# State-space scan layer: the gate's PSUM read moved from VectorE to ScalarE, its multiply to GpSimd, and the output projection from step 7 to step 9

## The reference

```python
xi, z = split(xs @ W_in)                 # 64 + 64 channels
xc = silu(causal_conv4(xi) + conv_b)
dt_r, B, C = split(xc @ W_x)             # 2, 16, 16
dt = softplus(dt_r @ W_dt + b_dt)
def step(h, inp):                        # h: 64 channels x 16 states
    h = exp(dt * A) * h + dt * B * x
    y = sum_over_states(h * C)
y = y + xc * D_skip
y = y * silu(z)                          # the gate
out = x + y @ W_out                      # the output projection and the residual
```

## Time and profile before

| | |
|---|---|
| time, median of 3 runs | 3292.82 us (3287.38 to 3304.67) |
| the profiled execution's own time | 3303.62 us |
| its span | 3301.8 us |
| its mean granted PE clock | 0.936 |
| busy share of the span | PE 81%, DVE 76%, POOL 60%, ACT 58% |

### The profile page before, as it was taken

One profiled execution on the slowest core, in us unless ns is written; L12 is line 12 of the kernel. 1 busy time (PEld: TensorE's weight loads), 2 busy tenths in 40 slices (PEclk: granted clock), 3 DMA queues, 4 the chain that ended last, 5 costly groups with the idle time before them and its releaser, 6 DMA issues.

```text
span 3301.8 us, 39492 instructions
## 1 busy us (share of the span) xinstructions
PE 2664.9 (81%) x12378; PEld 799.5 (24%) x12378; DVE 2516.6 (76%) x2227; ACT 1904.1 (58%) x2344; POOL 1989.3 (60%) x1216
## 2 busy tenths in 40 slices
PE   4888878888788875468888888887888888888886
PEld 1233122331223311122222222222222222222221
DVE  4555545555555443349999999999999999999998
ACT  2524545245462333276767777776777777676772
POOL 1444233442335420248787888878788887878886
PEclk9989989899899987779999999999999999999998
DMA  3588315883138855556767676776757676676865
GB/s 139 191 285 245 101 39 160 291 253 116 52 124 292 259 148 128 120 116 157 168 144 175 141 176 148 162 165 149 172 140 180 144 168 160 152 169 142 183 140 118
DMA packets 276832, 537.44 MB, mean 163 GB/s; under 512 B 60024, under 2 KB 171072, under 8 KB 275824
## 3 DMA queue, kind: packets, MB, share of 16 engines
q1 hardware_dynamic: 242208, 450.82, 52.4%
q0 software_dynamic: 17568, 59.00, 6.5%
q10 hardware_dynamic: 16944, 26.17, 3.2%
HBM read 396.55 MB, written 139.33 MB: 162 GB/s over the span
## 4 chain that ended last, share of the span: by engine, by line
issue 17%; PE 17%; DVE 16%; ACT 3%; DMA 2%; POOL 1%; DVEq 0%; ACTq 0%; POOLq 0%; SPq 0%
DVE m_pb L420 10%; PE m_pb L270 5%; PE m_py L253 5%; DVE m_hs L425 4%; PE m_misc L218 3%; PE m_misc L237 2%; ACT m_da L377 1%; DMA m_dtb<-dt_rows 1%; PE m_misc L224 1%; PE m_py L249 1%; DVE m_gated L407 1%; DMA dt_rows<-m_dt 1%; ACT m_xg L300 1%; POOL m_hs L451 0%; DVEq L424 0%
## 5 line engine op out<-in xcount | busy, mean ns | idle before, releaser
L451 POOL TENSOR_TENSOR m_hs<-m_hs,m_cs 128x1024 f32<-128x1024 f32 x512 | 1205.5, 2359 | 343.1 <-DVE m_hs L425 343.1
L425 DVE TENSOR_TENSOR_SCAN m_hs<-m_da,m_pb 128x1024 f32<-128x1024 f32 x512 | 1170.7, 2287 | 31.6 <-ACT m_da L377 6.5
L270 PE MATMUL m_pb<-m_dtx,late 64*128 64x512 f32 x2048 | 597.8, 649 | 217.7 <-DVE m_hs L425 217.2
L377 ACT ACTIVATE m_da<-m_dtb,m_a_neg 128x1020 f32<-128x1020 f32 x512 | 579.7, 1143 | 286.2 <-DMA m_dtb<-dt_rows 189.5
L420 DVE TENSOR_TENSOR m_pb<-m_pb,m_bs 128x1024 f32<-128x1024 f32 x512 | 620.5, 1212 | 33.6 <-PE m_pb L270 33.3
L253 PE MATMUL m_py<-m_hs,late 128*64 128x512 f32 x2048 | 566.3, 632 | 62.3 <-POOL m_hs L451 62.3
L1372 POOL TENSOR_TENSOR t_xc<-t_xc,big 128x512 f32<-128x512 f32 x96 | 119.2, 1266 | 409.4 <-DVE big L1278 409.4
L1148 ACT ACTIVATE t_sq<-t_bank 128x512 f32<-128x512 f32 x192 | 105.5, 595 | 371.1 <-PE t_bank L1013 370.7
L270 PEld LDWEIGHTS m_pb<-m_dtx,late 64*128 64x128 f32 x2048 | 168.0, 188 | 614.2 <-DVE m_hs L425 546.4
L1252 DVE SCALAR_TENSOR_TENSOR t_xc<-t_bank,t_vec,t_xc 128x512 f32<-128x512 f32 x96 | 72.1, 751 | 283.1 <-PE t_bank L967 283.1
L948 PE MATMUL t_bank<-late,t_lwin 128*128 128x256 f32 x816 | 226.1, 414 | 52.8 <-ACT big L1163 34.7
(11 more groups left out here) (152 smaller groups left out, 3670.8 us busy)
## 6 DMA issues: line engine op xcount, KB each, us to landing
m_dtb<-dt_rows SPq DMA_DIRECT2D x512, 512.0 KB, 6.1
late<-right_factor POOLq DMA_DIRECT2D x102, 512.0 KB, 5.4
right_factor<-t_tile SPq DMA_DIRECT2D x192, 256.0 KB, 2.9
t_tile<-band_out SPq DMA_DIRECT2D x183, 256.0 KB, 4.1
band_out<-t_vwin SPq DMA_DIRECT2D x48, 512.0 KB
band_out<-t_vwin SPq DMA_DIRECT2D x48, 480.0 KB
dt_rows<-m_dt ACTq DMA_DIRECT2D x64, 256.0 KB, 3.3
t_xc<-in_x_cm SPq DMA_DIRECT2D x4, 2048.0 KB, 14.6
```

Source lines behind the costliest of these rows:

```text
L270: m = nc.tensor.matmul(pb[s % 2][:, half(n)], spread[rows, dg, :], dtx[par][rows, half(q)], start=True, stop=True)
L377: nc.scalar.activation(da[:, s % DA_RING, :, 1:T], dtb[s % DTB_RING][:, :].rearrange("p (r t) -> p r t", t=T)[:, :, 1:T], ACT.Exp, scale=a ...
L425: nc.vector.tensor_tensor_scan(hs[:, s % H_RING, :], da[:, s % DA_RING, :, :].rearrange("p r t -> p (r t)"), pb[s % 2][:, :], 0.0, ALU.mul ...
L451: nc.gpsimd.tensor_tensor(hs[:, s % H_RING, :], hs[:, s % H_RING, :], cs[q][:, :], ALU.mult).then_inc(hc_ready, 1)
```

## The change

The gate is cut in two. ACT copies the sums out of PSUM into `gated` ("take0" after its step 12, "take1" after step 4 of the next chunk), and POOL multiplies `gated` in place by silu(z) (gate0 after its step 13, gate1 after step 5 of the next chunk). A new semaphore `y_taken` links the two, and skip(0) on PE waits for it instead of `y_gated`. DVE no longer gates. PE's out moves from step 7 to step 9, behind bq0, and DVE's fin from step 8 to step 10. skip(1) still stands at PE's step 11 and still waits for `fin_done`.

```diff
         SHARES = {
             "tensor": {0: [(PRE, "x")], 2: [(OWN, "bq1")], 4: [(OWN, "cq1")], 5: [(PRE, "dt")], 8: [(PRE, "z")],
-                       7: [(POST, "out")], 9: [(PRE, "bq0")], 11: [(PRE, "cq0")]},
-            "scalar": {1: [(PRE, "silu_x")], 3: [(OWN, "bq1")], 5: [(OWN, "cq1")],
+                       9: [(PRE, "bq0"), (POST, "out")], 11: [(PRE, "cq0")]},
+            "scalar": {1: [(PRE, "silu_x")], 3: [(OWN, "bq1")], 4: [(POST, "take1")], 5: [(OWN, "cq1")],
...
-                       8: [(PRE, "sp_back"), (PRE, "sp_relu")], 9: [(PRE, "silu_z")], 10: [(PRE, "bq0")], 12: [(PRE, "cq0")],
+                       8: [(PRE, "sp_back"), (PRE, "sp_relu")], 9: [(PRE, "silu_z")], 10: [(PRE, "bq0")], 12: [(PRE, "cq0"), (OWN, "take0")],
...
-            "vector": {4: [(POST, "gate1")], 8: [(POST, "out")], 11: [(OWN, "gate0")]},
-            "gpsimd": {7: [(PRE, "loss0"), (PRE, "log0")], 8: [(PRE, "dt0"), (PRE, "loss1")],
+            "vector": {10: [(POST, "out")]},
+            "gpsimd": {5: [(POST, "gate1")], 13: [(OWN, "gate0")], 7: [(PRE, "loss0"), (PRE, "log0")], 8: [(PRE, "dt0"), (PRE, "loss1")],
...
                             if q == 0:
-                                pe.wait_ge(y_gated, 2 * k - 1)
+                                pe.wait_ge(y_taken, 2 * k - 1)
                             else:
                                 pe.wait_ge(fin_done, k)
...
+                def take(k, par, q):
+                    a.wait_ge(hc_used, S * k + DG * (q + 1))
+                    if q == 0 and not early(k, 1):
+                        a.wait_ge(o_ready, k)
+                    nc.scalar.copy(gated[:, half(q)], py[q][:, :]).then_inc(y_taken, 1)
...
-                    v.wait_ge(misc_used[q], use(k, "z") + 1)
-                    nc.vector.tensor_tensor(gated[:, half(q)], py[q][:, :], act[par][:, W + q * HALF:W + (q + 1) * HALF],
-                                            ALU.mult).then_inc(y_gated, 1)
...
+                def gate(k, par, q):
+                    g_.wait_ge(y_taken, 2 * k + q + 1)
+                    g_.wait_ge(misc_used[q], use(k, "z") + 1)
+                    nc.gpsimd.tensor_tensor(gated[:, half(q)], gated[:, half(q)], act[par][:, W + q * HALF:W + (q + 1) * HALF],
+                                            ALU.mult).then_inc(y_gated, 1)
```

More of the change, by code:

```diff
@@ L129, in mamba_layer @@
                  "b_ready", "da_ready", "u_done", "h_ready", "hc_ready", "hc_used",
-                 "y_gated", "o_ready", "fin_done", "stored")
+                 "y_taken", "y_gated", "o_ready", "fin_done", "stored")
         (xg_ready, sp_abs, sp_exp, sp_relu, sp_ln, sp_sum, sp_act_done, sp_loss, sp_log, dt_ready, dtx_ready,
          b_ready, da_ready, u_done, h_ready, hc_ready, hc_used,
-         y_gated, o_ready, fin_done, stored) = map(sem, names)
+         y_taken, y_gated, o_ready, fin_done, stored) = map(sem, names)
         misc_ready = [sem(f"misc_ready{i}") for i in range(2)]
@@ L290, in _ @@
                 a.wait_ge(shared.x_in, shared.X_LOADS)
+                def take(k, par, q):
[3 more added lines that the diff above has]
+                    nc.scalar.copy(gated[:, half(q)], py[q][:, :]).then_inc(y_taken, 1)
                 def pre(k, par, op):
-                    if op in ("xg0", "xg1"):
+                    if op == "take0":
+                        take(k, par, 0)
+                    elif op in ("xg0", "xg1"):
                         q = int(op[2])
@@ L389, in post @@
                 def post(k, par, op):
+                    if op == "take1":
+                        return take(k, par, 1)
                     a.wait_ge(fin_done, k + 1)
@@ L398, in _ @@
             def _(v):
[L399 to L405, removed]
-                    v.wait_ge(misc_used[q], use(k, "z") + 1)
-                    nc.vector.tensor_tensor(gated[:, half(q)], py[q][:, :], act[par][:, W + q * HALF:W + (q + 1) * HALF],
-                                            ALU.mult).then_inc(y_gated, 1)
-                def pre(k, par, op):
-                    gate(k, par, 0)
                 def steps(k, par, s, first, last):
@@ L428, in post @@
                 def post(k, par, op):
[L429 to L440, removed]
+                    v.wait_ge(o_ready, k + 1)
+                    if not early(k, 1):
+                        v.wait_ge(stored, 16 * G * k)
+                    nc.vector.tensor_tensor(fin[:, :].rearrange("p (n t) -> p n t", n=SUB),
+                                            py[1][:, :].rearrange("p (n t) -> p n t", n=SUB),
+                                            xm[:, :, bass.ds(SUB * k, SUB)].rearrange("p t n -> p n t"),
+                                            ALU.add).then_inc(fin_done, 1)
+                schedule(v, "vector", None, steps, post)
             @block.gpsimd
@@ L452, in steps @@
                                             ALU.mult).then_inc(hc_ready, 1)
+                def gate(k, par, q):
[3 more added lines that the diff above has]
+                                            ALU.mult).then_inc(y_gated, 1)
                 def pre(k, par, op):
+                    if op == "gate0":
+                        return gate(k, par, 0)
                     q = int(op[-1])
@@ L470, in pre @@
                         nc.gpsimd.tensor_tensor(dtx[par][:, cols], dt[:, cols], act[par][:, cols], ALU.mult).then_inc(dtx_ready, 1)
-                schedule(g_, "gpsimd", pre, steps, lambda *_: None)
+                schedule(g_, "gpsimd", pre, steps, lambda k, par, op: gate(k, par, 1))
             @block.sync
```

## The result

The changed kernel takes 3341.59 us (median of 4 runs, 3339.1 to 3345.34) against 3294.4 before (median of 4 runs, 3287.38 to 3304.67): 47.2 us more, a ratio of 1.0142 (95% interval 1.0113 to 1.0171). The forecast was slower, 3324, with a range of 3276 to 3352. The direction, the mechanism and its place hold; the price of the clock was too small.

A forecast was written before the change was run, and what follows sets the result against it. The prediction took DVE as the bound. Its terms, -37.5 + 30 x 0.76 + 44.6 + 1.2, gave +31.1 us: 3334.7 against the profiled 3303.6, so 3324 for the median, with a range of 3276 to 3352.

The forecast's parts named there:

- DVE sets the pace, and the gates are worth 37.5 us.: Scan layer: DVE is the bound, so 63 gates of 0.595 us leaving it save 37.5 us.
- Copies on ACT and multiplies on POOL are free.: Each chunk: ACT's two 0.589 us copies and POOL's 1.268 us multiplies lie in idle time, adding nothing.
- fin moves behind the point where PE needs it.: PE waits 3.27 us for fin ahead of skip(1), making DVE wait 0.76 us ahead of mul(12), in 30 chunks.
- The clock: 27 x 1.65 = 44.6 us.: PE's work from skip(1) to b(12): clock falls after the idle wait, 1.65 us more in 27 chunks, 44.6 us.
- the chain of 3.0 us fits: Chunk 31 has no cq0, so PE's chain behind skip(1) takes 3.0 us and DVE does not wait.
- low clock for longer: Rival, 0.05: all four pieces behind skip(1) run at 1.2 GHz, 8.08 us instead of 4.04, every chunk: 3400 us.
- ACT's chain behind cq0 adds nothing.: From cq0's copies through dt_rows to b(1): stores run ahead in ACT's queue, 0 added; otherwise 1.0 us per chunk.
- the zero slack ahead of mul(1): After the chunk's end, b(1) ends at 2429.62 and mul(1) starts at 2429.67, leaving no slack.
- The end of the kernel.: After the last sum, a copy and a POOL multiply replace one DVE gate: +1.2 us.
- The sum: Whole kernel: -37.5 + 30 x 0.76 + 44.6 = +29.9, and +1.2 at the end, together +31.1 us.

The follow-up runs named there:

- e6_x_split: The changed kernel with projection and fin back in PE step 7 and DVE step 8, and the convolution's halves spread over PE steps 0 and 1: 3254.48 us, 0.9874.
- e4_fill: The changed kernel with cq0's two matmuls issued three times more between b(11) and skip(1), their result overwritten: 3285.88 us, 0.9969.
- e1: The changed kernel with only fin moved, from behind DVE's step 10 to behind step 9: 3271.25 us, 0.9925.
- e2: The changed kernel with projection and fin back in PE step 7 and DVE step 8, only the gate staying on ACT and POOL: 3266.03 us, 0.9919.
- e5_cq0_first: The changed kernel with cq0's matmuls issued ahead of skip(1) instead of behind sum(8): 3305.73 us, 1.0029.
- e9_cq0_first_fill: e5_cq0_first with cq0's two matmuls issued twice more ahead of cq0, their result overwritten: 3267.77 us, 0.9934.

## Why the prediction came out as it did

*DVE sets the pace, and the gates are worth 37.5 us.* Right. With nothing late, a chunk falls from 57.62 to 56.34 us (e6_x_split), 1.28 per chunk where 1.19 was worked out, and 39.7 in 31 chunks.

*Copies on ACT and multiplies on POOL are free.* Right. They take 0.592 and 1.266 us in the changed kernel (0.589 and 1.268 worked out), and doubling the copies changes nothing. The Trainium skill's rule on elementwise work ("GPSIMD Engine Reference", section 4.1) is right about the ratio, 1266 ns against 667, but the ratio did not set the time.

*fin moves behind the point where PE needs it.* Right, to a tenth of a us. Worked out were 3.27 us of waiting ahead of skip(1) and 0.76 us ahead of mul(12) at full clock; measured are 3.17 and, in e4_fill, 0.69.

*The clock: 27 x 1.65 = 44.6 us.* This is the term that was mis-sized. DVE waited 83.5 us in 31 chunks, and 30 x 0.69 = 20.7 of that is fin's place. The other 62.8 are the clock; 2.6 of them fell in chunk 31, where the forecast had said that the chain of 3.0 us fits: it took 6.0 us, at a granted clock of 0.50. Two things were missing. The clock fell in all 30 chunks, not 27. And in 10 of them it stayed low for about twice as long, so that the chain took about 6.9 us instead of 5.6. I had this as a rival ("low clock for longer"), but as a case for every chunk, at 0.05, instead of one that mixes with the forecast. The bound of the term, 1.65 for each of 30, was therefore no bound: it came from chains that had met one such stretch of low clock.

*ACT's chain behind cq0 adds nothing.* Right. ACT's timeline of the changed kernel, against the earlier trace rows:

```profile
2421.27 1.07 ACT L377 COPY m_cs<-m_misc 128x512 f32<-128x512 f32 x2 [7.87 <-PE m_misc L237]
2421.91 0.33 ACTq L402 DMA_DIRECT2D out_cm<-m_fin  x1
2422.22 0.61 ACT L296 COPY m_gated<-m_py 128x512 f32<-128x512 f32 x1
...
2422.70 1.17 ACT L385 ACTIVATE m_da<-m_dtb,m_a_neg 128x1020 f32<-128x1020 f32 x1
...
2423.75 1.29 ACT L308 ACTIVATE m_xg<-big,m_gn_bias,m_gn_scale 64x512 f32 x1
2423.88 1.25 ACTq L343 DMA_DIRECT2D dt_rows<-m_dt  x2
2425.06 1.28 ACT L308 ACTIVATE m_xg<-big,m_gn_bias,m_gn_scale 64x512 f32 x1
2426.36 1.15 ACT L385 ACTIVATE m_da<-m_dtb,m_a_neg 128x1020 f32<-128x1020 f32 x1
```

The first store is issued at 2421.91, ahead of six ACT instructions that come earlier in the program and are not yet done (a copy, take0, two decays, two of line 308). So ACT's queue holds at least these six, more than the four that the forecast named as the most in its rows. This agrees with the eight of the Trainium skill ("Advanced Engine Details and Errata", Engine Queue Depths). `dt_rows` is issued 1.74 us after mul(12), where 1.67 stood before. But the zero slack ahead of mul(1), which the forecast named, did cost once mul(12) was in time: 0.39 and 0.37 us per chunk on average in e1 and e2, inside the half us that the expectation for e1 allowed.

*The end of the kernel.* Right. From PE's last sum to the last gate:

```profile
3326.72 1.97 PE L253 MATMUL m_py<-m_hs,late 128*64 128x512 f32 x4 [2.26 <-POOL m_hs L444]
3328.74 0.58 ACT L296 COPY m_gated<-m_py 128x512 f32<-128x512 f32 x1 [19.77 <-PE m_py L253]
3329.40 1.26 POOL L450 TENSOR_TENSOR m_gated<-m_gated,m_act 128x512 f32<-128x512 f32 x1 [2.74 <-ACT m_gated L296]
```

The copy and the multiply take the place of one gate of 0.67 us there: +1.2. From the last scan's start to the last fin's start DVE's timeline has 9.55 us before (3287.74 to 3297.29) and 10.78 after (3321.96 to 3332.74), 1.23 more.

*The sum* with the measured waits, and the gates as they were worked out, is -37.5 + 83.5 + 1.2 = +47.2, and the medians differ by 47.2. That they agree to a tenth is luck. With the gates as measured, 39.7, the sum is +45.0. And the waits were read in profiled executions that differ by only 3337.3 - 3301.8 = 35.5 us. There, DVE's first scan of the layer starts at 1446.71 us before and at 1438.16 after, 8.6 us earlier, although the change touches nothing ahead of it. From that scan to the last fin the timelines have 1850.6 us before and 1894.6 after. This difference, 44.0, is what the 45.0 should be held against, and the terms explain it to about 1 us. Of the 16.1 us between the forecast sum of +31.1 and this +47.2, the clock term accounts for 18.2, and the term for fin's place (22.8 worked out, 20.7 measured) for -2.1.

## What to carry to other kernels

When a consumer's release moves later in a saturated engine's program, look up the first instruction elsewhere that waits for it, and count what is queued behind that one up to the next thing that the saturated engine needs; here one step decided between 0.9925 and 1.0142. If the engine that is made to wait is PE, look at the granted clock behind the wait: here the idle time was paid a second time in the work that followed, at 1.2 GHz instead of 2.4, and that was three quarters of what DVE waited. Before a move is given up, try its halves: the gate's move was worth 29 us, the projection's cost 73.

## What the runs showed of the hardware

- After 3.17 us without a matmul PE's granted clock fell in every chunk, and in 10 of 31 it stayed low through most of the 6.9 us of work behind the wait (0.57 over one of them). After 2.33 us in e5_cq0_first it fell in 29 of 31 chunks; after 2.28 us in the kernel before, in 19 of 30; after 1.21 us in e2_out7_fin8, in none of 30. So nearly the same length of idle time (2.28 and 2.33 us) did not give the same frequency. What sets it was not settled; the chunks' period differs (57.62 and 57.97 us), and that may be it, but no run varied the period alone.
- Matmuls whose result is thrown away, placed in a wait, made the changed kernel 56 us faster (e4_fill), and e5_cq0_first about 31 us faster (e9_cq0_first_fill: 0.9934 against 1.0029). The medians of these two, 3267.77 and 3305.73, lie 38 us apart, but the runs of the kernel before beside them differ by 4.
